# A two-layer decoder on one core: the loop over pairs of sequences written out on four engines

## What is computed

```
x = x + L0_attn(norm(x))           # windowed attention: 32 heads, 8 key heads, rotary positions, sinks
x = x + L0_xattn(norm(x), ctx)     # cross attention: 16 heads of 16, rms-normed queries and keys
x = x + L0_ffn(norm(x))            # router over 64: the best 8 weigh a bias row each
x = x + L1_attn(norm(x))           # 32 query heads on 8 key heads of 8, and a memory read
x = x + L1_xattn(norm(x), ctx, ctx)# mixing whose weights are a sum over all 16 sequences
x = x + L1_ffn(norm(x))            # 8 experts, the best 2 for every token
return x
```

## Time and profile before

| what | before |
|---|---|
| median of three runs | 1799.27 us |
| lowest and highest | 1796.6 and 1800.41 us |
| the profiled execution | 1792.72 us |
| its span, first to last instruction | 1790.9 us |
| mean granted TensorE clock | 0.804 |
| busy: PE, DVE, ACT, POOL | 1337.4, 1263.8, 657.0, 213.6 us |

### The profile page before, as it was taken

How to read it: one execution, slowest core, us unless ns; L and a number is a source line. 1 busy time by engine, 2 the same in 40 slices (tenths; PEclk the granted TensorE clock), 3 DMA queues, 4 the chain that set the end, 5 groups by cost and what they waited for, 6 DMA issues and landing times.

```text
span 1790.9 us, 37468 instructions
## 1 busy us (share of the span) xinstructions
PE 1337.4 (75%) x14566; PEld 1008.9 (56%) x14566; DVE 1263.8 (71%) x2529; ACT 657.0 (37%) x1533; POOL 213.6 (12%) x375
## 2 busy tenths in 40 slices
PE   4777877687778777877787778776877756649996
PEld 2665566556556655665556556655665544426664
DVE  5977697769776967696769676967796758743332
ACT  3334333433353334333433343235333433224432
POOL 1010001000100010001000100010000003533333
PEclk9896788678867886888788868887888668869998
DMA  9910000000000000000000000000000035223332
GB/s 318 333 59 1 20 3 1 1 19 3 1 1 19 3 1 1 19 3 1 1 20 3 1 1 19 3 1 1 8 2 1 1 125 196 103 72 57 61 60 39
DMA packets 51245, 70.82 MB, mean 40 GB/s; under 512 B 4912, under 2 KB 46576, under 8 KB 49520
## 3 DMA queue, kind: packets, MB, share of 16 engines
q1 hardware_dynamic: 43904, 58.83, 10.3%
q0 software_dynamic: 7152, 9.38, 3.2%
HBM read 34.52 MB, written 33.67 MB: 38 GB/s over the span
## 4 chain that ended last, share of the span: by engine, by line
issue 67%; PE 15%; DVE 9%; POOL 4%; ACT 2%; DMA 1%; SPq 0%; POOLq 0%; DVEq 0%
PE ps L946 12%; POOL rstd L1388 3%; POOL rstd L1387 1%; PE ps L950 1%; PE ps L495 1%; DVE experts L706 1%; ACT big L1307 1%; DVE ptf L1565 1%; PE ps L1048 1%; DMA sinkT<-in_sinkT 1%; PE ps L468 1%; DVE experts L707 0%; DVE ptf L670 0%; DVE bst L670 0%; DVE st L1644 0%
## 5 line engine op out<-in xcount | busy, mean ns | idle before, releaser
L1307 ACT ACTIVATE big<-ps,st 128x128 f32<-128x128 f32 x768 | 204.9, 406 | 205.9 <-DVE st L1646 205.9
L1048 PE MATMUL ps<-ident,big 128*128 128x128 f32 x1024 | 186.0, 350 | 34.6 <-ACT big L1307 18.2
L1565 DVE TENSOR_TENSOR ptf<-ps,ptf 128x1024 f16<-128x1024 f32 x128 | 154.5, 1221 | 67.7 <-ACT ptf L1313 66.3
L1048 PEld LDWEIGHTS ps<-ident,big 128*128 128x128 f32 x1024 | 165.0, 187 | 61.6 <-ACT big L1307 31.7
L1387 POOL TENSOR_TENSOR rstd<-mv,eps 128x1 f32<-128x1 f32 x80 | 18.3, 228 | 1261.8 <-DVE mv L1456 1261.8
L1313 ACT ACTIVATE ptf<-ps 128x1024 f16<-128x1024 f32 x128 | 130.6, 1029 | 92.8 <-PE ps L1048 92.6
L1644 DVE TENSOR_REDUCE st<-ps 128x8 f32<-128x1024 f32 x96 | 117.0, 1218 | 35.5 <-PE ps L946 35.5
L946 PE MATMUL ps<-wo,qhl 128*128 128x256 f32 x512 | 117.9, 384 | 16.2 <-DVE qhl L1570 13.9
L946 PEld LDWEIGHTS ps<-wo,qhl 128*128 128x128 f32 x512 | 94.9, 190 | 33.2 <-issue 17.4
L946 PE MATMUL ps<-experts,ptf 128*128 x312 | 100.7, 385 | 0.0
L1293 ACT ACTIVATE qhl<-big 128x1024 f16<-128x1024 f32 x32 | 33.8, 1057 | 163.3 <-DVE big L1530 160.9
(11 more groups left out here) (341 smaller groups left out, 3426.2 us busy)
## 6 DMA issues: line engine op xcount, KB each, us to landing
scratch<-blank SPq DMA_DIRECT2D x10, 1950.0 KB, 19.1
big<-in_gu SPq DMA_DIRECT2D x8, 1024.0 KB, 5.2
ptf<-scratch SPq DMA_DIRECT2D x39, 130.0 KB, 2.1
kf<-in_dn SPq DMA_DIRECT2D x8, 512.0 KB, 6.3
xin<-in_x SPq DMA_DIRECT2D x16, 128.0 KB, 2.3
cin<-in_ctx SPq DMA_DIRECT2D x16, 128.0 KB, 2.9
big<-in_wq SPq DMA_DIRECT2D x2, 1024.0 KB, 8.4
wo<-in_wo SPq DMA_DIRECT2D x1, 2048.0 KB, 13.8
```

The source lines that it names most:

```text
L1048: m = pe.transpose(ps_f(u, j // 4, P, (j % 4) * P), big[u][:, j * P:(j + 1) * P], ident[:])
L1307: m = f(big[u][:, c], ps_all[u][:, c], ACT.Exp, scale=scale, bias=st32[u][:, 3, j:j + 1])
L1565: S(u, tt(pt_l[u][:, c], ps_all[u][:, c], pt_h[u][:, c], ALU.subtract), f"pt{n}l{h}")
```

## The change

In all_turns the hardware loop becomes a loop of Python: the body is issued seven times one behind the other, with `it` a number. The values that waits compare with become constants everywhere, and the calls of enter and leave, which served the register, go. The order of the stages, the buffers, the semaphores and SP's loop stay as they are.

```diff
-    with eng.Fori(0, TURNS - 1) as it:
-        own.enter(it)
+    for it in range(TURNS - 1):
         for u, ahead, name in order:
             turn[u] = it + 1 if ahead else it
             stages[name](u)
-        own.leave(TURNS - 1)
     for u, ahead, name in order:
         if not ahead:
             turn[u] = TURNS - 1
```

## The result

The changed kernel takes 1786.14 us (median of five runs, 1781.66 to 1788.39), the kernel before beside it 1796.6 us (1793.85 to 1800.41). The ratio is 0.9938 with an interval of 0.9922 to 0.9953: 8.4 to 14.0 us less. Run again beside later experiments it gave 1788.31 us against 1796.5 us, 0.9947 (0.993 to 0.9964): 6.5 to 12.6 us less. The forecast was 1791.7 us, 7.6 us less: the direction and the range (1784.5 to 1796.5) hold, the size is on the small side. It started from the 1799.27 us of the first three runs; 2.7 of the 5.6 us by which it lies above 1786.14 are that base. The two profiled executions, 1792.72 and 1784.33 us, differ by 8.4 us, and their spans by as much (1790.9 and 1782.5 us).

A forecast was written before the change was run, and what follows sets the result against it. No engine was full; DVE was taken to idle after each of six jumps back to the loop's head. 16.9 - 6 x 1.54 = 7.6 us, other terms 0, off 1799.27 us gave 1791.7 us, range 1784.5 to 1796.5 us.

The forecast's parts named there:

- What bounds the kernel, and DVE's six jumps: DVE's idle time before the loop body's first instruction, 16.9 us in six waits, falls to 1.54 us each: 7.6 us gained.
- Whether the gain lasts: DVE's earlier start is kept through the turn, as in the straight-line last turn; the 31 us with "+" items count as unchanged.
- Registers at nothing: DVE's 693 register instructions, 27.7 us in all or 4.0 us a turn, run behind other work: no gain.
- PE's jumps at 0 of 0 to 1.8 us: PE's six jumps, 3.5 us in the median, are covered by matmuls issued before; 0 taken, at most 1.8 us of gain.
- The clock at 0, bounds 4.9 us of gain and 3.5 us of loss: Turn lengths vary with PE's granted clock; all seven like the shortest or the longest give the bounds, the mean is 0.
- the sentence on moving places: With turns shortened from 177.5 to about 176.2 us, the places in a turn at which the clock falls will move.
- How code is supplied, at 0: Straight-line code on PE might arrive late, one stop in each of eight turns, 24 to 31 us of loss; 0 taken.
- The rival "slower": Code comes late at PE's small score matmuls, a stop of 2.96 to 3.86 us a turn: 1815 to 1823 us, chance 0.07.
- The rival "the loop costs only its branch": Each DVE jump costs only its 63 ns branch, 0.4 us for six: 1798.9 us, chance 0.06.

The follow-up runs named there:

- the idle work: Changed kernel with 2.8 us of idle work on DVE ahead of the body's first instruction in turns 1 to 6, no jump: 1799.58 us, ratio 1.0013.
- The kernels with the moved jump: Kernel before, loops kept, DVE's body begun where DVE waits 3.8 us for PE: 1797.05 us; with code also shifted by eight semaphore instructions: 1793.05 us.
- the near jump: Changed kernel with a two-pass loop over one semaphore instruction ahead of the body's first instruction on DVE in turns 1 to 6: 1788.41 us, ratio 0.9954.
- the loop with the spread writes: Kernel before with SP alone written out and its ten scratch-clearing writes moved to the middle of turns 0 to 4: 1792.84 us, ratio 0.9987.

## Why the prediction was right

- **What bounds the kernel, and DVE's six jumps** (7.6 us by the sum): right. The wait fell to 1.54 us at the start of turns 2 to 7 in the first profile; in the second it is 1.54 and 2.0 us in turn, always ended by ACT's copy. From the start of turn 0 to that of the last turn the profiles are 7.4 and 10.3 us shorter than the one of before, and 7.3 us with DVE alone written out.
- **Whether the gain lasts** through the turn, read from the last turn: right for the items that turn has. L1573 comes 51.29 us after L1472 (1150.22 - 1098.93) and L1750 145.2 us (1244.11), against 51.29 and 144.13 in the earlier trace rows. The rest of the turn with its "+" items, counted as unchanged, takes 31.33 us (1275.44 - 1244.11), against 31.41 at the loop's exit (1282.73 - 1251.32).
- **Registers at nothing:** right within 0.2 us a turn, by the turn of the idle work laid on that of the loop. The kernels with the moved jump leave a doubt.
- **PE's jumps at 0 of 0 to 1.8 us:** right. PE's 32 matmuls now run through:

```profile
1141.41 7.14 PE L944 MATMUL ps<-wo,qhl 128*128 128x256 f32 x32 [1.31 <-DVE qhl L1568]
```

- **The clock at 0, bounds 4.9 us of gain and 3.5 us of loss:** within the bounds, and the term that came out furthest from its size. With the jumps taken off, the mean turn was 176.2 us before; it is 176.1, 175.8 and, with DVE alone written out, 176.1 us: over six turns 0.8, 2.6 and 0.6 us less. The turns settle in other patterns, as the sentence on moving places said, but the sum gave that no sign, and the turns scatter more than the forecast's 175.5 to 176.7 us: 174.96 to 176.95 in the first profile. That it is the clock is a reading, as above. How the 7.6 us become 10.5 in the first medians is not placed further: turn 0 and the part behind the last turn's start differ by 1.1 and 5.5 us between the two profiles of the changed kernel. The second interval has the 7.6 us in it, the first just misses it.
- **How code is supplied, at 0:** nearly right. The stops in the first turn stayed and no turn of PE got a new one above 0.5 us (the largest is 0.44). But DVE, which the prediction didn't name here, has two small ones now, 0.52 us at 209.54 (0.15 is usual) and 0.20 us at 365.99. The rival "slower" was real as a mechanism, but its stops of some 3 us came only where the DMA engines were full (share 1.06 and 1.09), which no later turn of the changed kernel is.
- **The rival "the loop costs only its branch"** is refuted by the near jump beside the far one: both take some 60 ns as a branch, and the far one makes L1474 1.2 to 1.4 us later.

## To carry to other kernels

Look for idle time in front of the first instruction of a loop's body with no releaser, and compare it with the same instruction where the loop falls through; the difference times the jumps is the first estimate of what writing it out is worth, where that engine's lateness is on the path: PE's 1.8 us were worth nothing. Go by the length of the wait and not by the name beside it: in the loop with the spread writes five of the six waits, as long as ever (2.73 to 2.80 us), are put down to ACT's copy, which ended 0.9 us before. Write out the engine whose jump delays the path and leave the others; but take the place of the jump as no free choice, since hiding it gained nothing here. A small change in a turn can cost more than itself (0.60 us of delay made turns 1.1 to 1.4 us longer here), so measure it over whole runs.

## What was not expected of the hardware

A branch back over a few instructions took some 60 ns on DVE, and the next instruction started 0.2 us after it did; one back over the whole body left DVE idle for 2.73 to 2.95 us, where 1.54 us is the wait without it. Writing the turns out made the traffic of code less, not more: the page's instruction queues moved 131 and 58 packets before, and now:

```profile
q8 instruction: 118, 1.93, 0.4%
q14 instruction: 43, 0.34, 0.1%
```

Straight-line code can be late: PE stood still for 3.85 us at a DMA share of 1.09 and for 3.05 us at 1.06, each time in the run of small matmuls, with a packet of code moved inside the stop. And turns of the same work repeat at one length for several turns (177.45 to 177.55 us) or alternate between two (175.28 and 176.28 us), with different clocks granted in the same stretch.
